# Seven PSUM banks in two rings, by the engine that empties them

## The reference: what is computed

```
x = x + layernorm(attention(layernorm(x)))      # layer 1: 16 heads of width 8, rope, causal softmax
x = x + layernorm(ffn_block(layernorm(x)))      # layer 2, below
```

## Time and profile before

| what | value |
|---|---|
| three runs | 576.18, 578.37, 578.45 us (median 578.37) |
| the profiled execution | 578.05 us, its span 576.0 us |
| busy TensorE / VectorE / ScalarE / GpSimd | 507.3 / 412.2 / 313.7 / 200.6 us |
| granted TensorE clock, mean | 0.984 |

### The profile page before, as it was taken

How to read it: one execution, slowest core, us unless ns; L and a number is a source line. 1 busy time by engine, 2 the same in 40 slices (tenths; PEclk the granted TensorE clock), 3 DMA queues, 4 the chain that set the end, 5 groups by cost and what they waited for, 6 DMA issues and landing times.

```text
span 576.0 us, 9488 instructions
## 1 busy us (share of the span) xinstructions
PE 507.3 (88%) x3168; PEld 276.7 (48%) x3190; DVE 412.2 (72%) x1209; ACT 313.7 (54%) x586; POOL 200.6 (35%) x268
## 2 busy tenths in 40 slices
PE   7888988978899888999999999998989798899784
PEld 3433443433443344556565556554756346553643
DVE  6689898798589976876686688766476764554465
ACT  2485685767656775656756646543355342654131
POOL 5432643365236541564336414421032000410010
PEclk9999999999999999999999999999999899999978
DMA  5455524114223432448345542532203200000001
GB/s 139 128 147 172 149 82 138 43 44 135 77 80 117 155 72 90 91 115 171 103 99 108 121 127 91 129 46 52 53 15 66 55 2 1 20 2 0 2 1 37
DMA packets 29672, 47.17 MB, mean 82 GB/s; under 512 B 4648, under 2 KB 15144, under 8 KB 29112
## 3 DMA queue, kind: packets, MB, share of 16 engines
q1 hardware_dynamic: 28496, 45.72, 31.0%
q10 hardware_dynamic: 1128, 0.85, 0.7%
HBM read 27.22 MB, written 18.87 MB: 80 GB/s over the span
## 4 chain that ended last, share of the span: by engine, by line
PE 54%; DVE 27%; ACT 10%; issue 5%; POOL 3%; DVEq 0%; ACTq 0%; POOLq 0%
PE ps L612 11%; PE ps L565 9%; DVE ps L1231 8%; PE ps L686 8%; PE ps L532 6%; PE ps L530 4%; PE ps L820 3%; DVE NM L1221 3%; DVE terms L1337 2%; PE ps L550 2%; ACT PG L853 2%; PE ps L559 2%; PE ps L737 2%; PE ps L667 1%; DVE stats L1205 1%
## 5 line engine op out<-in xcount | busy, mean ns | idle before, releaser
L853 ACT ACTIVATE PG<-ps 128x512 f32<-128x512 f32 x320 | 179.4, 600 | 139.0 <-PE ps L565 87.7
L1231 DVE CUSTOM_DVE_ANT_0 ps<-ps,below 128x512 f32<-128x512 f32 (+1 forms) x256 | 157.1, 638 | 45.2 <-PE ps L532 22.6
L565 PE MATMUL ps<-QS,K 128*128 128x512 f32 x320 | 115.4, 445 | 3.0 <-ACT PG L853 2.9
L612 PE MATMUL ps<-PG,V 128*32 128x512 f32 (+3 forms) x1024 | 95.0, 444 | 3.1 <-DVE ON L1278 1.8
L532 PE MATMUL ps<-K,QS 96*128 96x256 f32 (+3 forms) x256 | 74.1, 341 | 10.2 <-DVE NM L1231 9.9
L1221 DVE TENSOR_REDUCE NM<-ps 128x2 f32<-128x512 f32 (+1 forms) x96 | 65.5, 692 | 22.1 <-PE ps L550 18.3
L530 PE MATMUL ps<-KS,QS 96*128 96x256 bf16 (+3 forms) x256 | 64.5, 303 | 17.3 <-DVE NM L1231 13.2
L565 PEld LDWEIGHTS ps<-QS,K 128*128 128x128 f32 x320 | 53.9, 189 | 44.1 <-ACT PG L853 23.1
L1066 POOL TENSOR_TENSOR rstd<-ve,half 128x4 f32<-128x4 f32 x20 | 20.4, 1018 | 117.4 <-DVE ve L1213 83.2
L1174 POOL TENSOR_SCALAR_AFFINE_SELECT PG<-PG 128x512 f32<-128x512 f32 x64 | 39.6, 641 | 57.4 <-ACT PG L853 57.0
L1167 POOL TENSOR_SCALAR_AFFINE_SELECT PG<-PG 128x512 f32<-128x512 f32 x64 | 38.7, 638 | 49.5 <-ACT PG L853 49.5
(11 more groups left out here) (170 smaller groups left out, 679.4 us busy)
## 6 DMA issues: line engine op xcount, KB each, us to landing
scr<-QC SPq DMA_DIRECT2D x24, 512.0 KB, 2.8
QS<-scr SPq DMA_DIRECT2D x64, 128.0 KB
scr<-room SPq DMA_DIRECT2D x20, 256.0 KB, 2.6
QS<-scr SPq DMA_DIRECT2D x15, 288.0 KB
KS<-scr SPq DMA_DIRECT2D x15, 288.0 KB
QS<-scr SPq DMA_DIRECT2D x64, 64.0 KB
x<-in_x SPq DMA_DIRECT2D x4, 256.0 KB, 3.3
out_x<-x SPq DMA_DIRECT2D x3, 256.0 KB, 2.3
```

What stands on the lines that cost most here:

```text
L565: mm = pe.matmul(bank.rearrange("p (h q) -> p h q", h=HG), keys[:, SEQ[n] % 2, P * j:P * j + P], QS2[:, heads, P * i:P * i + P], start=(ke ...
L612: mm = pe.matmul(out, v, p, start=(j == 0), stop=(j == NT - 1), skip_group_check=True)
L853: act.activation(PG[:, n % 2, unit_place(LAYER[n], (u + k) % UNITS), :], ps[:, ST0 + (u + k) % 3, :], ACT.Exp, scale=scale).then_inc(exp_d ...
L1231: dve.tensor_tensor_reduce(out=bank[:, 0:w], in0=bank[:, 0:w], in1=below[:, T - w:T], scale=-1.0, scalar=-NEG, op0=ALU.add, op1=ALU.min, a ...
```

## The change

Banks 0, 6, 1 and 7 form a ring for whatever VectorE empties: fills and the side products that it reads. Banks 2, 3 and 4 form a ring for whatever ScalarE empties: units and the side products that it reads. A new generator `written()` lists all writers in TensorE's order; from it come each writer's bank (`BANK_OF`) and the writer that held the bank before (`HOLDER`), and one function `bank_free` waits for that holder alone. The lists for the ten first uses, for the last sequence's experts (`LAST_BANKS`) and bank 5 stay. The waits for all first uses of banks 0 to 4 at the start of the groups go, since `HOLDER` covers them. `y3part` asks for its bank at part 0.

```diff
-BANK, PRE_BANKS = [], (6, 7, 0, 1, 2, 3, 4, 6, 7, 1)
-for _u in range(_n[0]):
+PRE_BANKS, LAST_BANKS = (6, 7, 0, 1, 2, 3, 4, 6, 7, 1), (6, 7, 0, 1, 2, 3)
+DVE_RING, ACT_RING = (0, 6, 1, 7), (2, 3, 4)
+READ_BY_ACT = ("turnmax", "x1T", "v1", "o1T", "o1y", "x2T", "latv", "o2T", "x3T")
...
+def written():
+    for n in range(-3, LAST + 1):
+        for hh in range(HG):
+            for i in range(4):
+                if 0 <= n < NG and i < 2 + hh % 2:
+                    yield "unit", n * UNITS + 5 * (hh // 2) + 2 * (hh % 2) + i, True
+                if -2 <= n < NG - 2 and i < fills_of(hh)[1]:
+                    yield "fill", (n + 2) * FILLS + fills_of(hh)[0] + i, False
+            for m, h, stage, b, part in BESIDE:
+                if (m, h) != (n, hh):
+                    continue
+                if stage == "y3part" and part == 0:
+                    yield "side", BANK0["y3", b, 0], False
+                elif stage != "y3" or b < B - 2:
+                    takes = "ropeA2" if stage == "ropeA" and part % 2 else stage
+                    for k in range(TAKES.get(takes, (0,))[0]):
+                        yield "side", BANK0[stage, b, part] + k, stage in READ_BY_ACT
...
+for _kind, _u, _act in written():
...
+    else:
+        _ring = ACT_RING if _act else DVE_RING
+        _bank = _ring[_rings[_act] % len(_ring)]
+        _rings[_act] += 1
+    BANK_OF[_kind, _u], HOLDER[_kind, _u], _last[_bank] = _bank, _last.get(_bank), (_kind, _u)
...
+            def bank_free(kind, u):
+                before = HOLDER[kind, u]
+                if before is not None:
+                    held, v = before
+                    if held == "fill":
+                        pe.wait_ge(fill_read, v + 1)
+                    elif held == "unit":
+                        pe.wait_ge(exp_done, v + 1)
+                    else:
+                        pe.wait_ge(*was_read(v))
+                return ps[:, BANK_OF[kind, u], :]
...
-                if f >= 2:
-                    pe.wait_ge(fill_read, f - 1)
-                bank = ps[:, f % 2, :]
+                bank = bank_free("fill", f)
...
-                        for k in range(ST0, ST0 + 3):
-                            pe.wait_ge(bank_read[k], PRE_BANKS.count(k))
-                if u >= 3:
-                    pe.wait_ge(exp_done, u - 2)
-                bank = ps[:, ST0 + u % 3, :]
+                bank = bank_free("unit", u)
...
             def bank(u):
-                if USE[u]:
-                    pe.wait_ge(bank_read[BANK[u]], USE[u])
-                return ps[:, bank_of(u), :]
+                return bank_free("side", u)
```

More of the change, by code:

```diff
@@ L168, with fills_of @@
     _n = [a + t for a, t in zip(_n, TAKES.get(_takes, (0, 0, 0, 0)))]
-BANK, PRE_BANKS = [], (6, 7, 0, 1, 2, 3, 4, 6, 7, 1)
-for _u in range(_n[0]):
-    _k = _u - BANK0["o2T", B - 1, 0]
-    BANK.append(PRE_BANKS[_u] if _u < len(PRE_BANKS) else 4 if _u == BANK0["y3", B - 1, 0] else 6 + _u % 2 if _k < 0 else (6, 7, 0, 1, 2, 3)[_k % 6])
+PRE_BANKS, LAST_BANKS = (6, 7, 0, 1, 2, 3, 4, 6, 7, 1), (6, 7, 0, 1, 2, 3)
+DVE_RING, ACT_RING = (0, 6, 1, 7), (2, 3, 4)
+READ_BY_ACT = ("turnmax", "x1T", "v1", "o1T", "o1y", "x2T", "latv", "o2T", "x3T")
+def fills_of(hh):
+    return 2 * hh + hh // 2, 2 + hh % 2 + hh // 3
+def written():
[15 more added lines that the diff above has]
+                        yield "side", BANK0[stage, b, part] + k, stage in READ_BY_ACT
+BANK_OF, HOLDER = {}, {}
+_rings, _last = [0, 0], {}
+for _kind, _u, _act in written():
+    _k = _u - BANK0["o2T", B - 1, 0]
+    if _kind == "side" and _u < len(PRE_BANKS):
+        _bank = PRE_BANKS[_u]
+    elif _kind == "side" and _u == BANK0["y3", B - 1, 0]:
+        _bank = 4
+    elif _kind == "side" and _k >= 0:
+        _bank = LAST_BANKS[_k % len(LAST_BANKS)]
+    else:
[3 more added lines that the diff above has]
+    BANK_OF[_kind, _u], HOLDER[_kind, _u], _last[_bank] = _bank, _last.get(_bank), (_kind, _u)
+BANK = [BANK_OF["side", _u] for _u in range(_n[0])]
 USE = [BANK[:_u].count(BANK[_u]) for _u in range(_n[0])]
@@ L320, in block_program @@
         ps = ctx.enter_context(nc.psum_tensor("ps", [P, 8, T], F32))
-        ST0, BK_O = 2, 5
+        BK_O = 5
         loaded_first, loaded_qkv, loaded, x_loaded = sem("loaded_first"), sem("loaded_qkv"), sem("loaded"), sem("x_loaded")
@@ L533, in products @@
                                  stop=alone, skip_group_check=not alone)
-            def fills_of(hh):
-                return 2 * hh + hh // 2, 2 + hh % 2 + hh // 3
+            def bank_free(kind, u):
[9 more added lines that the diff above has]
+                return ps[:, BANK_OF[kind, u], :]
             def scores_for_max(n, hh, i):
@@ L635, in main @@
                         pe.wait_ge(consts_ready, CONSTS)
-                        for k in range(2):
-                            pe.wait_ge(bank_read[k], PRE_BANKS.count(k))
                 if n + 2 == 0 and hh == 2:
@@ L807, in y3 @@
                     return
-                bank(BANK0["y3", b, 0])
                 for part in range(5):
@@ L814, in y3part @@
                 pe.wait_ge(h_ready, 5 * b + part + 1)
-                dst = ps[:, BANK[BANK0["y3", b, 0]], :]
+                dst = bank(BANK0["y3", b, 0]) if part == 0 else ps[:, bank_of(BANK0["y3", b, 0]), :]
                 for t in range(NT):
@@ L852, in main @@
                         act.wait_ge(st_ready, u + k + 1)
-                        act.activation(PG[:, n % 2, unit_place(LAYER[n], (u + k) % UNITS), :], ps[:, ST0 + (u + k) % 3, :],
+                        act.activation(PG[:, n % 2, unit_place(LAYER[n], (u + k) % UNITS), :], ps[:, BANK_OF["unit", u + k], :],
                                        ACT.Exp, scale=scale).then_inc(exp_done, 1)
@@ L1226, in maximum @@
                 k = 2 * hh + hh // 2 + i
-                bank = ps[:, (n * FILLS + k) % 2, :]
+                bank = ps[:, BANK_OF["fill", n * FILLS + k], :]
                 if i < 2:
```

## The result

The changed kernel takes 546.44 us (median of 4 runs, 546.34 to 546.58), the old one 577.67 in the same comparison: ratio 0.9463, 95% interval 0.944 to 0.9485. That is 31.2 us, or 5.4%. The forecast was 564.0 with a range of 554 to 576: the direction held, the size was more than double, and even the rival "nearly the whole ceiling" (553) fell short.

The account below looks back on a forecast made before the run. TensorE was taken to bound layer 2 (91% busy) and to take turns with VectorE in layer 1; -4 - 6 - 4 - 1 + 1 = -14 us against 578.05 gave 564.0 us, range 554 to 576.

Parts of the forecast that it names:

- nearly the whole ceiling: Rival for the whole kernel: 25.5 us of waits and clock loss come back, giving 553 us; chance 13%.
- under 8: Sign for the fills: TensorE's waits on the maxima (L1231) fall from 23 us to under 8.
- term 2: Fills of layer 2: of 11.1 us of waits the ceiling is 10.2; gain taken 6 us, ends 0 and 11.1.
- Term 1: Fills of layer 1: of 13.4 us of TensorE waits, 40% carried; gain taken 4 us, ends 0 and 13.4.
- my last cut: Layer 1 fills: gain lowered from 5.4 to 4 us for a second path, ScalarE's normalisations and GpSimd's causal blocks.
- The worked cycle: One layer 1 cycle, waits from 70.22 us to the division at 78.29: 0.59 of 1.37 us kept, 43%.
- Term 3: Side products waiting for banks 6 or 7: half of 8.3 us, gain taken 4 us, ends 0 and 8.3.
- Term 4: Half clock from 452.31 to 455.73 us: gain taken 1 us if TensorE's idle wait before it shrinks, ends 0 and 1.6.
- the prediction's two readings: Clock dip near 452 us: goes with the wait, 1.6 us gained, or may stay or move, 0 gained.
- Term 5: ScalarE's ring, units sharing three banks with 68 products: loss taken 1 us, ends 0 and 19.
- Rival A: Waits return at L612 for the division, or for the tanh; only 4 us gained, 574 us; chance 17%.
- The sum: Whole kernel: gains of 4, 6, 4 and 1 us less a loss of 1 make -14 us, 564.0 us.

Follow-up runs that it names:

- e2: Changed kernel with the old wait of the fills (until the fill two before is reduced) put back in layer 1 alone: 557.22 us.
- e3: Changed kernel with the old wait of the fills (until the fill two before is reduced) put back in layer 2 alone: 559.70 us.
- e4: Changed kernel with a side product again waiting until the one two before it is read, fills and units as changed: 556.35 us.
- e8: Changed kernel with VectorE's division moved in front of the group's first maximum: 536.70 us.
- e12: Changed kernel with both old waits back, the fills' and the side products': 581.03 us against the old kernel's 578.85.
- e5: Changed kernel with ScalarE's side products put into VectorE's ring, units alone in banks 2, 3, 4: 552.06 us.
- e1: Changed kernel with every fill waiting again until the fill two before is reduced, in both layers: 570.96 us.
- e6: Changed kernel with three banks for VectorE (0, 6, 1) and four for ScalarE (2, 3, 4, 7): 559.06 us.

## Why the prediction was right in direction and wrong in size

- **That a fill's new condition is never later, and that no instruction is added.** Right as far as the traces show. The waits of L530 and L532 for the maxima (23 us, with the 1.4 on L1221 24.5) are gone, below the "under 8" that was to show it; those on L1430, L1547 and L1562 fell to 0.9 us. These 0.9 us are what is left of the old kernel's longest wait, 2.37 us at 450.69: the same fill now waits for the gate's signal, so 1.45 us of it are covered, where term 2 worked out 1.5.

```profile
424.55 0.50 PE L576 MATMUL ps<-K,QS 96*128 96x256 f32 x2 [0.92 <-DVEq L1589]
```

- **The step that failed: the base of terms 1 and 2.** They start from waits of 13.4 and 11.1 us, read from matmul rows alone; what a late matmul loses inside the busy time of the one before it was put at nothing. Of the 31.4 us of span, 16 came back as busy time. The idle time fell by 15 us, close to the 14 of the forecast. In each term a share was mis-sized besides, as follows.
- **Term 1, fills of layer 1: 4 us forecast, 10.8 measured (e2).** The 13.4 us to which I applied 40% was the idle time of matmul rows. Between 29 and 200 us the weight loads of the same fills had waited for L1231 for 38.3 us in 83 places, against 12.0 us in 25 places that I read the earlier trace rows. Of the 10.3 us of span that e2 loses, 5.1 are idle time, about the 5.4 ahead of my last cut, and 5.2 busy time. The worked cycle itself held: from one first values product to the next the old kernel takes 11.16 us (67.13 to 78.29), the changed one 10.55, so 0.61 us came back where 0.59 were to be kept, and the wait for the division is 1.26 us where 1.06 were forecast. But 10.8 is 81% of 13.4, so the 40% doesn't hold for the layer. Over the twelve groups from 54.56 to 201.81 us (50.12 to 189.83 in the changed kernel) 7.5 us came back where the matmul rows show some 12 us of waits for the maxima. One cycle was too small a sample, and the second cut, to 4, had no row behind it.
- **Term 2, fills of layer 2: 6 forecast, 13.3 measured (e3), above the end of 11.1 that I gave as the most.** The weight loads of L532 had waited 18.0 us in 27 places, the matmul rows 9.9 in nine. Of the 13.6 us of span that e3 loses, 7.6 are idle time and 6.0 busy time. So the cut to 6 for "paths beside it", with two late exponentials for evidence, was somewhat too deep, and the larger miss is again the busy part. Some of that is the clock's: e3 has two stretches at 1.2 GHz more than the changed kernel, at most 3.4 us.
- **Term 3, side products: 4 forecast, 9.9 measured (e4).** Visible waits of 8.3 us, halved without a row that asked for it; here the mis-sized part is idle time (8.9 us), so it is the halving that failed. I expected the tanh and the gate to take back what TensorE gained; they did not.
- **Term 4, the clock: a gain of 1 forecast.** Not confirmed. The dip at 452 us went with its wait, but the granted clock dropped in two other places, each behind a wait for the division. TensorE and the stretches by clock in the changed kernel (start:end, length, PE, PEld, DVE, ACT, POOL, clock, DMA):

```profile
116.65 1.94 PE L659 MATMUL ps<-PG,V 128*32 128x512 f32 x8 [1.26 <-DVE ON L1320]
...
454.56 1.93 PE L659 MATMUL ps<-PG,V 128*32 128x512 f32 x8 [1.85 <-DVE room L1320]
```

```profile
114.00:116.60 2.60, 1.39 (x7) 0.44 (x6) 2.57 (x8) 2.60 (x7) 2.60 (x4) 1.00 0.63 206
116.60:120.00 3.40, 3.35 (x15) 0.71 (x19) 3.30 (x14) 1.22 (x3) 3.14 (x4) 0.50 0.07 17
```

  The eight products at 116.65 take 1.94 us, where they take 1.07 at full clock. e8's profile, where the first of these waits is gone and the second is 1.22 us, has neither dip. But the waits alone don't explain them. In e4 TensorE waits for the same divisions for 1.26 us at 118.27 and 1.86 us at 464.74, and the clock stays up behind both:

```profile
464.74 1.06 PE L659 MATMUL ps<-PG,V 128*32 128x512 f32 x8 [1.86 <-DVE room L1322]
```

  The changed kernel's own 1.26 us at 72.68 has no dip behind it either. The Trainium skill ("TensorE: Matmul & The Clock Gate", "Part 1: The HAM clock gate") calls the lower clock the default, which activity releases. The dip that went from 452 us agrees with it, but why one wait is followed by a dip and its like is not stays open: of the prediction's two readings, the one in which the dip moves is the one that came.
- **Term 5, ScalarE's ring: a loss of 1 forecast, 2.2 measured by the medians (e12), within what the interval allows.** Right in kind. It priced the units alone, though: their waits for the exponential grew from 3.7 to 6.1 us, and ScalarE's side products wait 4.9 us for a bank of the ring (L724, L743), which the term leaves out.
- **Rival A** was half right. L612's wait on L1278 grew from 2.7 to 9.7 us, more than the 6 forecast, and moving the division brings 9.7 us (e8). But it took back only part: the 24.5 us for the fills are net of it. The lesson is that I used this wait to cut the gain, when it was a second gain in waiting.
- **The sum.** Five cautious factors of 0.4 to 0.75, mostly argued by another path close behind, were put on a base that left the busy part out. TensorE's visible waits that the change addresses added up to 32.8 us, and 31.2 came back. That the plain sum would have hit is luck: the idle time fell by 15 us alone, because waits returned at L612 and elsewhere, and 16 us of busy time, which the sum leaves out, filled the place. The idle time's 15 us against the forecast 14 is partly luck too: term 3 was 5 us short in it and term 4's gain did not come.

Open: how the gain of e8 divides between the shorter wait and the two dips of the clock that went with it (at most 3.4 of the 9.7 us by the estimate above), how much of this gain the old banks would give, and which ring ScalarE's side products are best put in, apart from the collision at the start in e5.

## What to carry to other kernels

Read a TensorE that waits for banks at its weight loads, in number and in length, not only at its matmul rows: here 75 of 116 late weight loads had no idle matmul row behind them, and half of what the fills' old wait cost was busy time. But don't add the weight loads' waits up as a price: they come to 61.7 us in e1, and removing them brought 24.5. When two engines pass buffers in turn and both are busy most of the time, as here (66 to 91%), try a third buffer first: it brought 20 of 24.5 us, the fourth 4.4; and count every product that shares the ring (e6), the first ones at the start too (e5). Once such a stall is gone, look at once for the next fixed meeting point of the same two engines: here a small reordering brought another 9.7 us.

## What the runs showed of the hardware that was not expected

A TensorE that executes the same matmuls at the same mean clock showed 16 us less busy time (507.3 to 491.0) when bank waits went; in the stretch compared above the matmuls only start closer together. And waits of TensorE of 1.26 and 1.85 us stood at the head of a stretch at the lower clock in the changed kernel, while another of 1.26 us in the same kernel (72.68), and those of 1.26 and 1.86 us at the same places in e4, had none: the length of a wait alone did not tell whether the clock would drop.
